# Layer 0's first pass: block 0's scores to exponentials placed ahead of iteration 1's keys, and the first row's DMAs dealt differently

## The reference

```python
ln_out = _ln(hidden_states, ln_w, ln_b)
q  = _ln(linear_fp8(ln_out, wq, ...), qln_w, qln_b)       # 2 heads of a group, 256 tokens
k  = _ln(linear_fp8(ln_out, wk, ...), kln_w, kln_b)       # 256 own tokens
v  = linear_fp8(ln_out, wv, ...)
qx = _ln(linear_fp8(ln_out, wqx, ...), qxln_w, qxln_b)
kx, vx = jnp.split(jnp.einsum('bsi,oi->bso', cond, w_kv_x), 2, axis=-1)   # 1601 context rows
kx = _ln(kx, kxln_w, kxln_b)
core = _gqa(q, k, v)          # softmax(q k^T / sqrt(d)) v over the 256 own tokens
xout = _gqa(qx, kx, vx)       # the same over the 1601 context rows
return einsum(fp8(concatenate([core, xout])), wproj)
```

## Time and profile before

| | us |
|---|---|
| median of 3 runs (1662.07 to 1662.55) | 1662.1 |
| the profiled execution | 1661.28 |
| its span, first to last instruction | 1659.4 |
| PE busy / DVE busy / ACT busy / POOL busy in the span | 1573.0 / 1375.4 / 1387.7 / 1145.9 |

### The profile page before, as it was taken

How to read it: one execution, slowest core, us unless ns; L and a number is a source line. 1 busy time by engine, 2 the same in 40 slices (tenths; PEclk the granted TensorE clock), 3 DMA queues, 4 the chain that set the end, 5 groups by cost and what they waited for, 6 DMA issues and landing times.

```text
span 1659.4 us, 43881 instructions
## 1 busy us (share of the span) xinstructions
PE 1573.0 (95%) x15804; PEld 999.3 (60%) x15996; DVE 1375.4 (83%) x3483; ACT 1387.7 (84%) x2346; POOL 1145.9 (69%) x1778
## 2 busy tenths in 40 slices
PE   3899999999999999999999999998898999999998
PEld 2567777777777677777777777766564333333333
DVE  8899999999999989999988999999897755556422
ACT  6889888888888788888888888875447999999997
POOL 5777888878787677887887888885775646646300
PEclk9899999999999999999999999999999999999999
DMA  5499999999999989999999999999323232212100
GB/s 190 124 203 202 198 190 206 201 209 209 195 205 214 206 194 188 229 210 219 201 193 228 206 216 198 203 192 244 102 46 112 47 74 52 47 34 47 34 14 14
DMA packets 609481, 261.12 MB, mean 157 GB/s; under 512 B 576624, under 2 KB 581744, under 8 KB 607856
## 3 DMA queue, kind: packets, MB, share of 16 engines
q1 hardware_dynamic: 605040, 258.05, 72.1%
q10 hardware_dynamic: 4224, 0.25, 0.2%
HBM read 99.15 MB, written 17.29 MB: 70 GB/s over the span
## 4 chain that ended last, share of the span: by engine, by line
PE 41%; DVE 7%; issue 4%; ACT 3%; DMA 1%; SPq 0%; DVEq 0%; ACTq 0%
PE pv L3037 9%; PE pv L1860 6%; PE score L1840 6%; PE pa L2987 4%; PE score L3017 2%; PE tb L1717 2%; ACT P L2925 2%; PE tb L1758 2%; PE tb L3017 1%; PE tb L1817 1%; PE pa L1791 1%; ACT praw L2925 1%; PE pa L1758 1%; DVE S L1301 1%; PE score L2202 1%
## 5 line engine op out<-in xcount | busy, mean ns | idle before, releaser
L1860 PE MATMUL pv<-PT,VV 128*128 128x256 bf16 (+1 forms) x2880 | 338.5, 274 | 9.7 <-DMA PT<-PB 8.2
L1589 ACT ACTIVATE PB<-S,rsum 128x1024 bf16<-128x1024 f32 (+1 forms) x256 | 246.4, 988 | 107.0 <-DVE rsum L1332 79.9
L1860 PEld LDWEIGHTS pv<-PT,VV 128*128 128x128 bf16 (+1 forms) x2880 | 279.6, 98 | 76.4 <-issue 36.6
L1840 PE MATMUL score<-KK,QT 128*128 128x512 bf16 (+2 forms) x1794 | 314.0, 318 | 10.4 <-DVE mxp L1301 2.7
L1323 DVE SCALAR_TENSOR_TENSOR PB<-S,rsum,PB 128x1024 bf16<-128x1024 f32 (+1 forms) x256 | 288.9, 1129 | 1.4 <-ACT PB L1589 1.4
L1840 PEld LDWEIGHTS score<-KK,QT 128*128 128x128 bf16 x1920 | 157.6, 98 | 140.6 <-DVE mxp L1301 9.6
L1579 ACT ACTIVATE S<-S,nmx 128x1601 f32<-128x1601 f32 x128 | 210.2, 1642 | 5.2 <-DVE nmx L1313 5.0
L2925 ACT ACTIVATE P<-score 128x1024 f32<-128x1024 f32 x196 | 198.0, 1054 | 1.9 <-PE score L3017 0.9
L1717 PE MATMUL tb<-stage,wsb 128*128 128x512 bf16 x767 | 148.1, 336 | 9.4 <-POOL stage L562 8.9
L3037 PE MATMUL pv<-P,V 128*9 128x256 f32 (+1 forms) x2288 | 152.2, 380 | 1.1 <-DVE pv L2308 0.8
L1127 POOL TENSOR_SCALAR S<-S,rsum 128x256 f32<-128x256 f32 x128 | 73.9, 577 | 107.6 <-DVE rsum L1332 95.3
(11 more groups left out here) (295 smaller groups left out, 3596.7 us busy)
## 6 DMA issues: line engine op xcount, KB each, us to landing
x<-rs_d SPq DMA_DIRECT2D x16, 936.0 KB, 5.1
rsb<-rs_d SPq DMA_DIRECT2D x16, 936.0 KB, 5.5
wsb<-w_split SPq DMA_DIRECT2D x46, 256.0 KB, 4.6
wsb<-w_split SPq DMA_DIRECT2D x23, 512.0 KB, 5.2
wpr<-in_wprojT SPq DMA_DIRECT2D x23, 512.0 KB, 6.6
context_d<-stage SPq DMA_DIRECT2D x16, 400.2 KB, 4.1
l_ctx<-context_d SPq DMA_DIRECT2D x4, 1601.0 KB, 7.4
rawh<-in_w_all SPq DMA_DIRECT2D x12, 512.0 KB, 5.3
```

The costliest lines, as they stand in the source:

```text
L1589: e.activation(m.PB[n % 2][:, 2 * a:a + b], m.S32[n % 2][:, a:b], ACT.Copy, scale=m.rsum[n % 2][:, 1:2]).then_inc(s["p_hi"], 1)
L1840: i = e.matmul(m.score[:, at:at + b - a], qt[:, kind, qp, q * P:(q + 1) * P], kk[:, kp, a:b], start=(k == 0), stop=(k == 2))
L1860: i = e.matmul(m.pv[:, at:at + 256], vv[0:rows, v, t, :], m.PT[k % 2][0:rows, turned(c, a), :], start=(c == first and r == 0), stop=(c == ...
```

## The change

Five things are altered, all in the first pass and at the start of iteration 0.

1. PE: `scores(0, 0)` comes right behind `turn_queries(0, 1)`, ahead of `values(0, 2)`, and `scores(0, 1)` behind `values(0, 3)`. Iteration 1's first queries and keys come behind both.
2. DVE: `scaled(0, 0)` comes ahead of the second half's `dve_context_low(1, 1)`; `scaled(0, 1)`, `scaled(0, 2)` and `offset(0)` come at the end of the first pass, ahead of iteration 1's query statistics and keys. `query_stats(0, 1)` comes four instructions earlier, `values_low` a little earlier too.
3. ACT: `exponentials(0)` comes at the end of the first pass, ahead of iteration 1's `keys_high`. `values_high(0, 0)` and `(0, 1)` come earlier, and the cast of the context's second half (`act_context_high(1, 1)`) ahead of `query_full(0, 1)`.
4. The DMA that deals out iteration 0's sums is issued by SP, not by ACT.
5. The store of group 0's weights comes behind the row's store and load on SP's queue.

```diff
@@ sp_prologue
     sp_load_context(e, m, s, 1, 1)
-    sp_store_weights(e, m, s, 0)
@@ sp_attention
+def deal_sums(e, m, s):
+    e.dma_start(m.ssc[:, :], m.sqs[0:SQG * R:R, :].rearrange("j (r c) -> j r c", c=SQC)).then_inc(s["sums_in"], 16)
...
+    e.wait_ge(s["sums_out"], 1)
+    deal_sums(e, m, s)
     row_out(0)
     row_in(0)
+    sp_store_weights(e, m, s, 0)
     sp_store_weights(e, m, s, 1)
@@ DVE
     dve_round(e, m, s, 3)
+    query_stats(0, 1)
     e.tensor_scalar(m.gate[:, 0:1], ...)
     e.reciprocal(m.rsmc[:, :], m.smc[:, :])
     dve_weights_low(e, m, s, 1, 0)
-    query_stats(0, 1)
     dve_weights_low(e, m, s, 1, 1)
     dve_context_low(e, m, s, 1, 0)
+    values_low(0, 0)
     dve_sum_weights(e, m, s, 1)
     dve_centre_weights(e, m, s, 1)
-    values_low(0, 0)
+    values_low(0, 1)
     dve_round_start(e, m, s, 4)
     dve_round_add(e, m, s, 4)
-    values_low(0, 1)
     dve_weights_low(e, m, s, 1, 2)
+    scaled(0, 0)
     dve_context_low(e, m, s, 1, 1)
     values_low(0, 2)
     values_low(0, 3)
+    scaled(0, 1)
+    scaled(0, 2)
+    offset(0)
...
-        scaled(4 * it, 0)
+        if it:
+            scaled(4 * it, 0)
...
-        scaled(4 * it, 1)
-        scaled(4 * it, 2)
+        if it:
+            scaled(4 * it, 1)
+            scaled(4 * it, 2)
         p_lo(4 * it - 1, 1)
-        offset(4 * it)
+        if it:
+            offset(4 * it)
@@ ACT, sums_out
-        e.wait_ge(s["sums_out"], it + 1)
         if it:
+            e.wait_ge(s["sums_out"], it + 1)
             e.wait_ge(s["kr_pow"], it)
-        e.dma_start(m.ssc[:, :], ...)
+            deal_sums(e, m, s)
@@ ACT, first pass
     act_context_high(e, m, s, 1, 0)
+    values_high(0, 0)
     for ic in range(IC):
         act_norm_weighted(e, m, s, ic)
     act_scaled_inputs(e, m, s, 4)
-    values_high(0, 0)
+    values_high(0, 1)
     query_norm(0, 1)
-    values_high(0, 1)
+    act_context_high(e, m, s, 1, 1)
     query_full(0, 1)
-    act_context_high(e, m, s, 1, 1)
     values_high(0, 2)
     values_high(0, 3)
     act_scaled_inputs(e, m, s, 5)
+    exponentials(0)
...
-        exponentials(4 * it)
+        if it:
+            exponentials(4 * it)
@@ PE
     turn_queries(0, 1)
+    scores(0, 0)
     values(0, 2)
     values(0, 3)
+    scores(0, 1)
 
     for it in range(NGB + LAG - 1):
+        queries(it + 1, 0)
         if it:
-            queries(it + 1, 0)
-        scores(4 * it, 0)
-        if it == 0:
-            queries(1, 0)
+            scores(4 * it, 0)
         keys(it + 1, 0)
-        scores(4 * it, 1)
+        if it:
+            scores(4 * it, 1)
```

More of the change, by code:

```diff
@@ L1554, in sums_out @@
         e.activation(m.sqs[:, :], bank_of(m, "SS")[:, 0:SQW], ACT.Copy, bias=D * EPS5).then_inc(s["sums_out"], 1)
-        e.wait_ge(s["sums_out"], it + 1)
         if it:
+            e.wait_ge(s["sums_out"], it + 1)
             e.wait_ge(s["kr_pow"], it)
-        e.dma_start(m.ssc[:, :], m.sqs[0:SQG * R:R, :].rearrange("j (r c) -> j r c", c=SQC)).then_inc(s["sums_in"], 16)
+            deal_sums(e, m, s)
     def projection_high(i):
```

## The result

The changed kernel's median is 1663.8 us (20 runs), the kernel before's in the same comparison 1661.8 us (20 runs): ratio 1.0014, 95% interval 1.0007 to 1.0020. That is 2.0 us slower by the medians and 2.3 by the ratio (interval 1.2 to 3.3), small but resolved, where the prediction had 1.1 us faster. The time lies in the predicted range, and the change is smaller than the 0.2% that the prediction took for the limit of a measurement; 20 runs did resolve it, and its direction is the wrong one. The profiled span grew from 1659.4 to 1661.8 us. The end of the first pass moved by +1.72 us (first product 78.98 to 80.70), the fourth group of squares (168 us) by +1.64, the fourteenth (511 us) by +1.65, later ones by 1.7 to 2.2. So 1.7 of the span's 2.4 us are there after the first 81 us; the rest comes behind the last squares (1096 us, +1.67), and its cause was not found.

The account below looks back on a forecast made before the run. PE bounds the loop from 90 us; DVE and ACT, nearly full, set much of the first pass. First pass -2.1 us, clock +1.0, sum -1.1: profiled 1660.2, forecast median 1661.0 us, range 1658.2 to 1664.2 (8 in 10).

Parts of the forecast that it names:

- the loop carries the shift: Loop from 90 us: runs at PE's pace, so the first pass's gain or loss reaches the end almost unchanged.
- rival B: Loop at 545 us: loses a slow-clock PE wait (1657.6, chance 0.08) or catches more (+2.4 or +5.8, chance 0.07).
- The deal and the store: First pass, DMA: the deal waited for the store; alone it takes 1.9 us, so POOL starts at 32.3, 2.4 earlier.
- Rival C: First pass, DMA: the deal needs its 4.3 us whoever issues it; 1662.7, chance 0.08.
- The row `rsb`: SP's queue: 4.5 us to landing, at 41.5; up to 2.5 later beside the store, counted only in the range.
- PE's second turn: First pass, PE: turn of the second queries starts at 39.65, 7.35 us after the deal lands.
- The sum for `scaled(0, 0)`: First pass, DVE: due at 42.4, from a start at 33.0 and step times of the kernel before.
- Slow stretch costs nothing before: PE's first slow-clock stretch, kernel before: cost nothing, since DVE came to the scores at 47.98 without a wait.
- The 1.0 us that it was to take back: First pass, changed kernel: DVE waits for scores on slow PE, taking 1.0 us of the 2.1 gained.
- nothing of block 0 stands between iteration 1's first and third keys: ACT: exponentials run 47.7 to 49.8, iteration 1's first keys follow 1.0 us earlier, with no block 0 work before third keys.
- Second keys' low part: DVE, iteration 1: ends at 55.8 for 57.92, 2.1 us earlier before the clock; near 57 in the changed profile.
- A: First pass, PE's clock: slow for 5.2 us and falling again before iteration 1's turn; +1.0, 1663.1, chance 0.22.

Follow-up runs that it names:

- e1: Kernel before, with only the deal issued by SP and group 0's store moved behind the row; ratio 0.9996 against the kernel before.
- e2: Changed kernel with deal and store put back (ACT issues, store in front), so only the new orders of PE, DVE and ACT; ratio 1.0014 against the kernel before.
- e3: Changed kernel with block 0's exponentials back behind iteration 1's second keys on ACT; ratio 1.0007 against the kernel before.
- e10: Changed kernel with DVE's low part of the weights moved into iteration 0 and block 0's exponentials back in their old place; ratio 1.0001 against the kernel before.
- e13: Kernel before, with only group 0's store moved behind the row, ACT still issuing the deal; ratio 0.9996 against the kernel before.
- e14: Kernel before, with only the deal's issue moved to SP, the store staying ahead of it; ratio 0.9995 against the kernel before.
- e9: Changed kernel with three of POOL's low parts cut to 8 columns, every order and wait kept; ratio 1.0008 against the kernel before.
- e4: Changed kernel with POOL's low part of the second context moved behind the second queries' low part; ratio 1.0010 against the kernel before.
- e5: Changed kernel with DVE's dve_weights_low(1, 2) moved from ahead of scaled(0, 0) into iteration 0; ratio 1.0007 against the kernel before.
- e7: Kernel before, with 22 idle products added in PE's wait ahead of the turn of the second queries; ratio 1.0052 against the kernel before.
- e6: Changed kernel with 22 idle products added in PE's wait ahead of the turn of the second queries; ratio 1.0067 against the kernel before.
- e11: Changed kernel with DVE's low part of the weights later and 22 idle products in PE's wait ahead of the second queries' turn; ratio 1.0067 against the kernel before.

## Why the prediction was wrong

**That the loop carries the shift** was right: +1.64 us from the fourth squares to the fourteenth, behind +1.72 at the first product. The 545 us event came at 546.95 (2.29 us of waiting, 24 products in 4.45 us) and added 0.5, most of it given back within one iteration; rival B did not decide. But its mechanism is real, and the loop is less rigid than this one shift suggests. In e1, e2, e3, e10, e13 and e14 the same 24 products took 2.78 us, and between the fourteenth and the sixteenth squares these loops gained 1.1 to 1.7 us on the kernel before. The loop of e1 stands 2.76 us ahead at 1096 us, with a first product only 0.45 ahead. So a difference of a microsecond in the first pass can't be read off the end of one execution.

**The deal and the store.** The cause was right, the size a little small: 2.26 us and not 1.9, and the issue itself came 0.4 later than at 30.4, so 33.04 and not 32.3. Rival C is false: moving the store away is worth 1.3 us (SP issues) to 2.1 us (ACT issues). The prediction's reading that the page's rule frees the deal does not hold either. The Trainium skill ("DMA: Bandwidth & Descriptors", Queues, rings and completion order) has a DMA engine change queues only at the end of a packet, and lets a typical packet hold 9 to 17 descriptors. The store is 1 MB in 128 rows of 8 KB; dealt out over 16 engines that is, as an estimate, 8 descriptors for each, which can fit into one packet, and then the deal has to wait by this rule too. The trace agrees: the deal's packets ran only behind the store's.
The row `rsb`, for which the sum took nothing, paid for the store beside it: it took 6.0 us to land and not 4.5, and was there at 37.25 + 6.0 = 43.25, not at 41.5.

**PE's second turn** came at 40.78 and not 39.65. 0.74 of it is the deal; the rest is what POOL's `a_rs` (1.47 us and not 0.19) cost net of other POOL steps that were shorter. It ends 0.04 us behind DVE's `stage` row beside it (36.45 + 1.23). The trace names DVE's `VV` as what ended PE's wait (40.73), but ACT's `kn` ended as long ahead of the turn as before (40.63, 0.15 us), so which of the two came last is open.

**DVE: the step that failed.** The sum for `scaled(0, 0)` was 33.0 + 10.82 + 1.14 - 2.60 = 42.4. Start (33.31) and order were right, the durations were not. The prediction took them from the kernel before. There most of these steps ran while POOL was busy with four-column steps or waited, and DVE idled (2.10 and 1.60 us) while POOL did its wide ones. The earlier deal and the new order slid wide POOL steps under them: +3.7 us by the rows, and 46.20 and not 42.4. e9 shows the cause (POOL cut down, 5.59 back to 2.16 us), e4 and e5 that moving one step on either side takes DVE's lateness away. DVE was late by 1.8 us only against the scores, which were done at 44.43: with short steps it would have waited for them and for the row (43.25), so 42.4 was out of reach in any case. The prediction treated the time of an instruction as its property, and asked of the shifted engines only whom they wait for.
What the rows show first is this: steps with all their inputs in SBUF grew (0.29 to 1.25, 0.28 to 0.65, 0.78 to 2.40), steps with an input in PSUM (`VV<-tb`) took 0.68 and 0.69 throughout, and three of the four long rows from 40.65 on end 0.15 or 0.16 us behind the POOL row beside them. The Trainium skill ("SBUF — State Buffer", SBUF: two separate sides) has GpSimd and DVE share a pair of ports that one holds for a whole instruction while the other stands still; on DVE's side it names instructions in a mode that uses two ports and those with two inputs in SBUF. By that rule, such a DVE step that starts second ends behind the POOL step. The trace agrees for three of the four long rows, by the 0.15 us above. `a_rs` (36.25) is a case the other way round: it starts while a DVE step with two such inputs runs (`wo<-wf,win,wo`, 34.95 + 1.58) and ends with the next one.

**The clock.** "Slow stretch costs nothing before" was wrong: e7 shows 1.0 us. The 1.0 us that it was to take back in the changed kernel was wrong as well: e6 shows nothing, because DVE came 1.8 us after the scores were done even at half speed. It costs something only once DVE is on time: with the weights' step later, `scaled(0, 0)` comes 11.46 us behind `rr<-ssc` in e5 and 10.83 in e11, where the clock was kept up.

**ACT.** That nothing of block 0 stands between iteration 1's first and third keys was true, but its price was not weighed: the exponentials stand ahead of `kn`, 6.18 us ahead of PE's turn. With exponentials at 47.7 the turn would have come at 53.9, 1.0 us earlier than before, and 11.17 + 12.1 us later the first product at 77.2. That is an estimate from the changed kernel's own distances, and no run here had exponentials earlier than 49.07; by it the prediction's order gains. At 51.28 it loses: the turn comes at 57.45. Before, `kn` did not depend on block 0 at all. So an uncertain term (DVE) had been put ahead of a step that until then had slack against it.

**Second keys' low part** ended at 58.45 + 0.74 = 59.2 and not near 57, the first product came at 80.70 and not at 77.9: most of what the exponentials were late (51.28 and not 48), carried on.

**The rivals.** A, slower than before through the clock (1663.1), and B with one more event (+2.4, 1664.5) came nearest to 1663.8 in time, and both had the wrong reason. For A: its fall of the clock at the third wait is real and was priced well (1.3; measured 1.33 to 1.67 in e11 and e4), but the changed kernel escapes it. For B: its loop caught no further event. That the measured time still fell into the range is luck, since no term of the range stood for what happened. No rival had DVE's steps themselves grow; it belonged there, as the mechanism that ends on the slow side.

## What to carry to other kernels

When an edit slides GpSimd's work under VectorE's, or the other way, do not carry durations over: look up which pairs lie side by side before and after, and add up the overlaps of SBUF-only steps. A step moved ahead on one engine delays everything behind it by its own lateness; ask what stood there before and did not depend on it. A stall that is filled or shortened may move a fall of the clock and not remove it, so read the granted clock behind every remaining wait.

## What was not expected of the hardware

- The same int16 step over 512 columns took 0.29 or 1.25 us, two steps of the weights 0.61 or 2.40 us, by what POOL did beside them.
- A 7.5 KB deal on another queue waited for a 1 MB store issued 0.12 us ahead of it: 4.32 us and not 2.20.
- With PE's waits of the same length at the same place (3.06 to 3.22 us) the clock fell in e4, e9 and e11 and stayed up in the changed kernel, e2 and e5. The fall costs 1.3 to 1.7 us there. What decides it was not found.
- 22 idle products in a wait at 34 us cost 6 to 9 us half a millisecond later. It stays open.
